# Attention output products on four column tiles, with a sum of four key tiles of P, in three groups for a pair of heads

## The reference

```python
scores = jnp.einsum('bhqd,bhkd->bhqk', Q, K) / scale
scores = jnp.where(causal, scores, jnp.float32(-jnp.inf))
attn = jax.nn.softmax(scores, axis=-1)
out = jnp.einsum('bhqk,bhkd->bhqd', attn, V)
```

## Time and profile before

| | us |
|---|---|
| median of the three timed runs | 758.27 |
| lowest, highest | 757.69, 768.73 |
| the profiled execution | 768.15 |
| its span, first to last instruction | 766.4 |

### The profile page before, as it was taken

The page is one execution under the profiler, slowest core; times in us unless marked ns, Lnnn a source line. Parts: engine busy times, 40 slices in busy tenths (PEclk is TensorE's granted clock), DMA queues, the critical chain, the costliest instruction groups (busy, mean ns, idle before and its releaser), DMA issues.

```text
span 766.4 us, 10665 instructions
## 1 busy us (share of the span) xinstructions
PE 743.2 (97%) x3563; PEld 539.6 (70%) x3563; DVE 438.5 (57%) x1103; ACT 307.4 (40%) x641; POOL 247.0 (32%) x224
## 2 busy tenths in 40 slices
PE   7999999989999999999999999999999999999996
PEld 7888888755555556566546547787788888888884
DVE  7978765895775767677767726773324114214112
ACT  3323132265664656566646564222332222223221
POOL 0815153311113141414231426932223223224223
PEclk9999999989999999999999999999999999999998
DMA  8677468643665666667656556670001001001001
GB/s 279 228 268 261 172 259 269 248 140 101 170 170 144 166 163 169 171 166 183 170 143 166 139 161 159 231 321 1 0 1 56 0 1 55 0 0 56 0 1 57
DMA packets 54318, 104.39 MB, mean 136 GB/s; under 512 B 14820, under 2 KB 18404, under 8 KB 53748
## 3 DMA queue, kind: packets, MB, share of 16 engines
q1 hardware_dynamic: 54264, 103.72, 44.3%
HBM read 69.62 MB, written 38.21 MB: 141 GB/s over the span
## 4 chain that ended last, share of the span: by engine, by line
PE 84%; DMA 4%; issue 4%; DVE 2%; POOL 2%; ACT 2%; SPq 1%; DVEq 0%; POOLq 0%; ACTq 0%
PE ps L1101 37%; PE ps L1240 17%; PE ps L1126 9%; PE ps L1316 9%; PE ps L1219 9%; DMA q_st<-neg_max_T 3%; PE ps L1093 2%; POOL hid_lo L592 1%; PE ps L1160 1%; ACT o_raw L687 1%; ACT p L680 1%; DMA l_cols<-o_raw 1%; SPq L421 0%; PE ps L1137 0%; DMA rec_l<-rec_rows 0%
## 5 line engine op out<-in xcount | busy, mean ns | idle before, releaser
L680 ACT ACTIVATE p<-ps 128x384 f32<-128x384 f32 (+3 forms) x384 | 160.7, 487 | 74.8 <-PE ps L1219 74.2
L841 DVE CUSTOM_DVE_ANT_0 masked<-ps,mask_qk 128x512 bf16<-128x512 f32 (+1 forms) x240 | 114.4, 503 | 80.3 <-PE ps L1126 79.0
L1219 PE MATMUL ps<-q_st,k_st 99*128 99x384 f32 (+2 forms) x384 | 136.4, 373 | 6.0 <-DMA q_st<-neg_max_T 4.9
L1240 PE MATMUL ps<-p,v_slot 128*64 128x512 f32 (+3 forms) x768 | 141.6, 506 | 0.2 <-ACT o_raw L687 0.2
L1126 PE MATMUL ps<-k_st,q_st 96*128 96x512 f32 (+2 forms) x384 | 132.3, 366 | 2.0 <-DVE row_max L841 1.7
L1052 DVE SCALAR_TENSOR_TENSOR hid<-ps,us_sb,silu 128x512 f32<-128x512 f32 x44 | 33.0, 751 | 165.3 <-PE ps L1101 159.6
L592 POOL TENSOR_TENSOR hid_lo<-hid,hid_hi 128x512 fp32r<-128x512 f32 x44 | 56.7, 1289 | 172.4 <-ACT hid_hi L756 172.4
L561 POOL TENSOR_SCALAR_AFFINE_SELECT p<-p 128x512 f32<-128x512 f32 x64 | 40.8, 642 | 215.4 <-ACT p L680 215.4
L1240 PEld LDWEIGHTS ps<-p,v_slot 128*64 128x64 f32 x768 | 51.3, 140 | 78.0 <-issue 65.4
L1126 PEld LDWEIGHTS ps<-k_st,q_st 96*128 96x128 f32 x384 | 72.7, 190 | 32.4 <-issue 21.8
L1219 PEld LDWEIGHTS ps<-q_st,k_st 99*128 99x128 f32 x384 | 72.9, 191 | 25.3 <-ACT p L680 8.9
(11 more groups left out here) (119 smaller groups left out, 1074.2 us busy)
## 6 DMA issues: line engine op xcount, KB each, us to landing
qk_scratch<-st_hi SPq DMA_DIRECT2D x32, 512.0 KB, 3.8
q_st<-qk_scratch SPq DMA_DIRECT2D x32, 384.0 KB, 4.4
k_st<-qk_scratch SPq DMA_DIRECT2D x32, 384.0 KB, 5.1
flag_st<-in_ffn SPq DMA_DIRECT2D x32, 264.0 KB, 2.8
ffn_copy<-in_ffn SPq DMA_DIRECT2D x32, 264.0 KB, 3.4
qk_scratch<-st_lo SPq DMA_DIRECT2D x16, 512.0 KB, 3.9
o_T<-o_raw SPq DMA_DIRECT2D x32, 128.0 KB, 4.8
rec_l<-rec_rows SPq DMA_DIRECT2D x32, 128.0 KB, 3.3
```

The source lines that it names most:

```text
L680: act.activation(p32[:, at:at + q0 + w - keep], ps[:, ST_BANK + i % ST_RING, keep - q0:w], ACT.Exp, scale=SCALE).then_inc(exp_done, 1)
L841: ins = dve.tensor_tensor_reduce((masked_a if u < 2 else masked)[:, s_before(i) % 2, col:col + kept], scores, mask_qk[:, 512 - kept:512], ...
L1219: pe.matmul(ps[:, ST_BANK + i % ST_RING, 0:w], k_st[0:K_ALL, slot, kt * P:(kt + 1) * P], q_st[0:K_ALL, slot, q0:q0 + w], start=True, stop= ...
L1240: ins = pe.matmul(ps[VW * a:VW * (a + 1), o_bank(u, half), q0 - 512 * half:512], v_slot[:, slot, kt, :], p32[:, at:at + n], start=(kt == 0 ...
```

## The change

Half 0 stays as it is (part 0). Half 1 is split into two parts of 256 queries, and each product is made with 32 weight columns on one of four column tiles: two for each head. The upper tile of a head ("v" rows) takes V with key tiles 0 to 3 (part 1) or 0 to 5 (part 2). The lower one (the rows that held the row sums) takes in columns 0 to 255 the row sums ("l": ones as weights), and in columns 256 to 511 V with the remaining key tiles ("w"). To make the row sums short, POOL adds the second half of P over the key tiles 0 to 3 of each head into `p_sum` (`sum_p`, three additions of 128x512), so one "l" product stands for four. The list of rounds sets the order; a round's products are meant for different tiles. Part 1 has 1024 columns on each of the four tiles, part 2 has 1536.

The three parts are three groups: after places 3 and 9 of the even step, and after place 6 of the odd step. ACT copies out three times for a pair. SP moves two more pieces for a pair (`o_w`, the "w" outputs), POOL adds them to o_T ahead of the scaling, and the reciprocal rows of a group are loaded into the place of group 7 in o_T (`rec_of`), so that SP has to wait for the scaling of group 6 before it moves the pair before the last. The load of Wo moves from stage A to step 30.

```diff
-PV_AFTER = ((3, 9), (3, 9))
+PV_AFTER = ((3, 9), (6,))
...
-PV_GROUPS = [[(0, 0), (0, 1), (0, 2), (0, 3)], [(1, 0), (1, 1)], [(1, 2), (1, 3), (1, 7)], [(1, 4), (1, 5), (1, 6)]]
+PV_GROUPS = [
+    (0, [[("vl", 0)], [("vl", 1)], [("vl", 2)], [("vl", 3)]]),
+    (1, [[("v", 0), ("w", 4)], [("v", 1), ("l", None)], [("v", 2), ("l", 4)], [("v", 3), ("l", 5)], [("w", 5)]]),
+    (2, [[("v", 0), ("w", 6)], [("v", 1), ("l", None)], [("v", 2), ("l", 4)],
+         [("v", 3), ("l", 5)], [("v", 4), ("l", 6)], [("v", 5), ("l", 7)], [("w", 7)]]),
+]
...
+        def o_bank(u, part):
+
+            return (O_BANK, ST_BANK + 2, ST_BANK)[part] if u == PAIRS - 1 else O_BANK
+
+        def rec_of(g):
+
+            return o_T[:, GROUPS - 1, :] if g < GROUPS - 1 else rec_last[:, :]
...
             def move_pair(u):
 
-                sp.wait_ge(o_evac, 2 * u + 2)
+                sp.wait_ge(o_evac, PARTS * (u + 1))
                 if u % 2 == 0 and u >= 2:
                     sp.wait_ge(l_out, 16 * (u // 2))
+                if u == PAIRS - 2:
+                    sp.wait_ge(o_scaled, GROUPS - 1)
...
+                    sp.dma_start(o_w[t // 4 % 2][rows, :], o_raw[l_rows, u % 2, S:S + 2 * QW]).then_inc(o_moved[u % 2], 16)
...
+                if t == HEADS - 2:
+                    sp.wait_ge(st_ps, NPC * t)
+                    sp.dma_start(wo_st[:, :, :], wo).then_inc(wo_in, 16)
...
             def scale_group(g):
 
                 pool.wait_ge(rec_in, 64 * (g + 1))
-                pool.tensor_tensor(o_T[:, g, :], o_T[:, g, :], rec_l[:, :], ALU.mult).then_inc(o_scaled, 1)
+                pool.tensor_tensor(o_T[:, g, S // 2:S], o_T[:, g, S // 2:S], o_w[g % 2][:, :], ALU.add).then_inc(o_joined, 1)
+                pool.wait_ge(o_joined, g + 1)
+                pool.tensor_tensor(o_T[:, g, :], o_T[:, g, :], rec_of(g), ALU.mult).then_inc(o_scaled, 1)
...
+            def sum_p(t):
...
+                total = p_sum[:, t % SUM_SLOTS, :]
+                if t >= SUM_SLOTS:
+                    pool.wait_ge(p_sum_read, 2 * ((t - SUM_SLOTS) // 2 + 1))
+                pool.tensor_tensor(total, second_half(0), second_half(1), ALU.add).then_inc(p_sum_step, 1)
+                pool.wait_ge(p_sum_step, 2 * t + 1)
+                pool.tensor_tensor(total, total, second_half(2), ALU.add).then_inc(p_sum_step, 1)
+                pool.wait_ge(p_sum_step, 2 * t + 2)
+                pool.tensor_tensor(total, total, second_half(3), ALU.add).then_inc(p_summed, 1)
...
             for t in range(HEADS):
                 copy_v(t)
                 if t % 4 == 0 and t >= 8:
                     scale_group((t - 8) // 4)
-                mask_p(t)
+                mask_low(t)
+                sum_p(t)
+                mask_high(t)
...
             def output_products(u, group):
 
+                part, rounds = PV_GROUPS[group]
                 if group == 0:
                     pe.wait_ge(exp_done, NPC * (2 * u + 1) + P_LOW + 1)
                     pe.wait_ge(v_copied, 2 * u + 2)
                     pe.wait_ge(p_low_masked, 2 * u + 2)
-                elif group == PV_HIGH:
+                elif group == 1:
+                    pe.wait_ge(p_summed, 2 * u + 2)
                     pe.wait_ge(p_high_masked, 2 * u + 2)
...
+                if group < PARTS and u == PAIRS - 1 and part > 0:
+                    pe.wait_ge(exp_done, NPC * HEADS)
+                elif group < PARTS and PARTS * u + part > 0:
+                    pe.wait_ge(o_evac, PARTS * u + part)
+                for products in rounds:
                     for a in range(2):
...
+                        for kind, kt in products:
+                            output_product(u, a, part, kind, kt)
```

More of the change, by code:

```diff
@@ L159, in transformer_block @@
             xst_c = sb("xst_c", [P, TJ, H], F32, after_wo)
-        wo_st = sb("wo_st", [P, KC, H], F32)
+        p_sum = sb("p_sum", [P, SUM_SLOTS, S // 2], F32)
+        o_w = [sb(f"o_w{k}", [P, S // 2], F32) for k in range(2)]
         with ExitStack() as after_v:
@@ L180, in transformer_block @@
         q_st = sb("q_st", [P, SLOTS, S], F32R)
+        with ExitStack() as after_two_k:
+            wo_st = sb("wo_st", [P, KC, H], F32, after_two_k)
         with ExitStack() as after_k:
@@ L273, in transformer_block @@
         p_high_masked = sem("p_high_masked")
-        pv_half = [sem(f"pv_half{k}") for k in range(2)]
+        p_sum_step = sem("p_sum_step")
+        p_summed = sem("p_summed")
+        p_sum_read = sem("p_sum_read")
+        pv_part = [sem(f"pv_part{k}") for k in range(PARTS)]
         o_evac = sem("o_evac")
@@ L1220, in shifted_piece, with output_product @@
                           start=True, stop=True).then_inc(st_ps, 1)
+            def output_product(u, a, part, kind, kt):
+                slot, bank = (2 * u + a) % SLOTS, o_bank(u, part)
+                q_end = S // 2 if part == 0 else S // 2 + QW * part
+                q_low = 0 if part == 0 else q_end - QW
+                q0 = q_low if kt is None else max(P * kt, q_low)
+                if kt is None:
+                    probs = p_sum[:, (2 * u + a) % SUM_SLOTS, q0 - S // 2:q_end - S // 2]
+                else:
+                    at = slot * P_SIZE + P_OFF[kt] + q0 - P * kt
+                    probs = p32[:, at:at + q_end - q0]
+                row = VW * a
+                if kind == "vl":
+                    rows, weights, col = slice(row, row + VW), v_slot[:, slot, kt, :], q0 - q_low
+                elif kind == "v":
+                    rows, weights, col = slice(row, row + D), v_slot[:, slot, kt, 0:D], q0 - q_low
+                elif kind == "l":
+                    rows, weights, col = slice(row + D, row + VW), v_slot[:, slot, 0, D:VW], q0 - q_low
+                else:
+                    rows, weights, col = slice(row + D, row + VW), v_slot[:, slot, kt, 0:D], QW + q0 - q_low
+                ins = pe.matmul(ps[rows, bank, col:col + q_end - q0], weights, probs,
+                                start=((kind, part, kt) in PV_FIRST), stop=((kind, part, kt) in PV_LAST), skip_group_check=True)
+                if kt is None and part == 2:
+                    ins.then_inc(p_sum_read, 1)
+                if (kind, part, kt) in PV_LAST and kind != "l":
+                    ins.then_inc(pv_part[part], 1)
             def output_products(u, group):
+                part, rounds = PV_GROUPS[group]
                 if group == 0:
```

95 lines of the change are left out of this document (49 added, 46 removed).

## The result

The changed kernel takes 772.11 us (median of 4 runs, 770.28 to 774.14) against 758.15 before: 1.0151 of it, with a 95% interval of 1.0109 to 1.0192. It is slower, by about 11.5 us by the ratio and 14 by the medians (one of the four executions of the kernel before took 768.73 us); the forecast was 755.5, a gain. A pair is measured between the transposes of the row maxima in PE's timeline; "13 pairs" are those between the fourth and the thirtieth transpose.

The account below looks back on a forecast made before the run. PE, busy for 97% of the span, was taken as the bound. The terms summed to -2.5 us for the profiled execution (765.7), -2.8 without late rows: 755.5 against the median of 758.27; range 738 to 775 for 8 in 10.

Parts of the forecast that it names:

- The products: PE's output products, parts 0 to 2: 7.02 us against 8.34, with one entry less 1.42 us saved a pair.
- The second rival: Four column tiles do not run at the pace of two, each round twice as long: about 805 us, chance 0.11.
- the estimate that stood beside it: From 2.38 times for three column tiles: rounds 1.26 times as long, 1.1 us a pair, some 771 us.
- third rival: POOL sets the pace: additions cost 1.75 us beside DVE and PE stands at part 1: 777 us, chance 0.12.
- The wait at the transpose: Odd step: PE stands 0.7 us a pair for DVE before the transpose, half that in pairs with a late row.
- its additions cost nothing: POOL's six additions a pair, 1.2 us each: sums ready with 2.7 us of cover, so the wait costs nothing.
- The pair of 17.8 us: Two heads in stage B were to take 17.8 us in place of 18.55.
- The end: Last products and start of stage C: products +1.2 us, end +5.0, clock +1.6; bounds of the whole 3 to 10.
- The products end 1.2 us later: Last products of stage B: PE stands 2.1 us for the sum of head 31, so they end 1.2 us later.
- The later chain: Last move issued 6.6 us after the products' end; reciprocals 3.8 us later, first product of batch 1 5.0 later.
- The late rows: Rows of maxima that PE waits for: SP's extra moves make the late ones 0.4 us later each, +2 in all.
- The clock: After PE's stand at the end, 3.7 us at 0.56 of the clock, as seen before: +1.6 us.

Follow-up runs that it names:

- e3: Changed kernel with each of POOL's three additions cut to 16 of 512 columns from head 3 on: 761.17 us, 1.0013 of the kernel before.
- e6: Changed kernel with the two small DVE instructions ahead of the transpose written as reductions, POOL's sums whole: 762.29 us, 1.0005 of the kernel before.
- e1: Kernel before with only the filler behind xT made 48 floats shorter, so buffers behind it lie 192 bytes lower: 766.79 us, 1.0079 of before.
- e5: Changed kernel with 192 bytes of small tiles allocated behind xT, restoring its distance to the weights modulo 2048: 766.84 us, 1.0060 of the kernel before.
- e4: Kernel before with three dummy POOL additions of 128x448 for each head, written to a tile nobody reads: 761.94 us, 1.0017 of before.
- e11: Kernel before with the two small DVE instructions ahead of the transpose written as reductions, as a control: 761.56 us, 0.9991 of before.
- e2: Changed kernel with the 64 bytes of neg_max allocated behind xT, so xT moves by 64 bytes: 772.8 us, 1.0158 of the kernel before.
- e8: Changed kernel with the three additions of the last head (31) on DVE in place of POOL: 767.89 us, 1.0061 of the kernel before.
- e9: Changed kernel with the edits of e5, e6 and e8 together: 750.85 us, 0.9866 of the kernel before.

## Why the prediction was wrong

**The products** were right. Parts 1 and 2 took 1.87 and 2.73 us, forecast 1.88 to 1.99 and 2.73 to 2.84. Four column tiles run at the pace of two, and the second pass of a short product waits for nothing. The second rival is out, and with it the estimate that stood beside it. By this estimate from the factor for three column tiles in the Trainium skill, "TensorE: Matmul & The Clock Gate", Part 3, "Measured speedup vs the span model", the two parts would have been some 1.1 us longer; no run shows this, and that the estimate's 771 is close to the measured time is chance. So it is with the third rival's 777: its additions of 1.47 us and more, for which PE would wait in every second pair, did not come.

**The wait at the transpose** was right in mechanism: 0.7 us from the order, which e3 measured at 0.70. POOL added 0.25.

**POOL: that its additions cost nothing was the step that failed.** The prediction worked out when a sum is ready and whether PE would wait for it ("the wait costs nothing"). That part held (additions 1.28 to 1.34 us, no wait for a sum but in the last pair). It did not ask what POOL's longer presence does to DVE, although its third rival had the rule in hand. It applied it one way only, as DVE slowing POOL, and to the weight test alone, although L859, on which the transpose waits, has two inputs from SBUF as well. The pair of 17.8 us that the text expected is the one that e3 and e6 show; with the hold it is 18.4, or 9.2 us in 13 pairs (239.8 less 230.6). The Trainium skill, "SBUF — State Buffer", "Who interferes with whom", says that a DVE instruction with two inputs from SBUF contends with a POOL instruction that reads SBUF, that in its two-port modes whoever issues first has the shared pair to its end, and that one with a single SBUF input outside these modes does not contend. This case agrees on the first and the last: from 161 to 581 ns with two inputs, and reductions that stay at 160. The second fits the multiplication, from 178 to 549, if it runs in such a mode, which no trace shows; which of the two engines began first is seen at 353.53 and 353.57 alone.

**The place in memory** was no term of the sum. The shorter filler stood in the diff and was passed over as bookkeeping; e1 prices it at 0.8%, e5 at 0.9%, 6 to 7 us. No row of the trace of before could have shown it.

**The end** was mis-sized in one term. "The products end 1.2 us later" became 4.5, because the stand was 3.85 us in place of 2.1 and the slow clock, forecast behind the last products, came inside them. The third of POOL's additions took 2.12 us and the mask behind it 1.62, where 1.3 and 0.64 are usual; DVE was at work on SBUF too (3.44 of 4.0 us from 453.2), all three of its instructions there, L1041 and L1049, with two inputs from SBUF; but what held POOL there was not tried. The later chain was right: the last move was issued 6.3 us after the products' end (forecast 6.6), and counted from there the reciprocals came 3.0 us later than before (forecast 3.8), the multiplication of group 7 began 4.3 us later and the first product of batch 1 came 4.1 us later (forecast 5.0).

**The late rows** were wrong in sign: PE waited 4.9 us for them in the earlier trace rows, and once, for 0.4, in the changed kernel. They were forecast to get worse by 2. In the profile of before they hold about 9 us over 13 pairs of 18.55 (250.5 less 241.2). The prediction took it that the executions near 758 have none; that was too simple. In e1, e4 and e11, which keep the old order, 13 pairs take 244.3 to 245.3 us and PE waits 1.9 to 2.7 us for rows, in e11 in an execution of 759.88. So ordinary executions of the kernel before lose 3 to 4 us to them, which the changed kernel hardly does. Why is open: e2, e5 and e8, which have the hold too, show no such wait, and e3, e9 and e6, nearly or wholly without it, 0.5, 1.3 and 3.0 us.

**The clock** of the stand was read too mildly: 0.56 of the full clock means that nearly the whole stretch ran at the lower of the two levels, not half of it. The 1.6 us taken from it do not depend on that.

Put together, from the forecast of 2.8 us less: the hold +9.2, memory +5.9, the end +1.1 (8.4 from the last transpose to the first product of batch 1, 7.3 forecast), rows -2, the pair without a hold 0.09 us quicker than worked out, -1.2. That makes +10.2, beside the +11.5 of the ratio. The closeness is in part luck: the 3 to 4 us of late rows that ordinary executions lost before are not in it, and with them it is some 7. The timed runs price the hold (e6, 1.5%) and the memory (e5, 0.9%) at 11 and 7 us, 3 more than these rows; what then remains is within their intervals and is not settled.

## What to carry to other kernels

When work is moved to POOL, list the DVE instructions that run beside it and ask of each whether it reads two SBUF tiles or is a plain multiplication: such instructions were held here, one of them for a whole POOL addition, and it matters where PE waits for them next. The remedy may be a different form of the DVE instruction and not less work on POOL. Buffers that change size move all that lies behind them, so the durations of instructions that the change does not touch are to be compared as well.

## What the runs showed of the hardware

- A TensorE product of 512 columns takes 227 ns from start to start or 233, and in the FFN with one shift (e2) 238 with xT_hi and 229 with xT_lo, by the distance in SBUF of its two operands: moving the weights (e1) costs what moving the other operand (e5) gives back. A shift of 192 bytes was worth 0.8 to 0.9% of this kernel.
- A DVE instruction on 8 columns took up to 1.24 us beside one POOL addition of 1.26, and ended with it; a reduction with as many results at the same place took 0.16 (e6). The masked maxima of 512 columns, with one input from PSUM and one from SBUF, kept their time beside the additions: 680 ns, 687 before.
- Four fp32 column tiles of 32 weight columns each, fed 256 columns a round, ran without a loss against two tiles of 64: 1.87 and 2.73 us for 1024 and 1536 columns, 1.87 for 1024 before.
